# Attention loop: values a step later, split maxima turned a step later still, weight pieces off GpSimd, threshold operations spread over groups

## The reference

```
attention, 32 heads of 16:
  x  -> chunks of 64 tokens; subtract (max+min)/2 per channel and chunk;
        8 scale classes by the channel maximum; round to int4
  Q, K, V = that @ int4 weights + bias;  probs = softmax(Q K^T);  ctx = probs V
  ctx -> the same chunks, thresholds (cmax > tmax / 2^k), classes, int4 rounding
  out = that @ int4 Wo + bias
cross attention with one energy matrix per batch (ctx_1024, Wq, Wk)
ffn: three matrices of 2048 x 512, each made ternary:
  w_int = clip(round(w / mean|w|), -1, 1);  down(silu(gate) * up)
```

## Time and profile before

| what | us |
|---|---|
| median of 3 runs | 1165.96 (1163.58 to 1167.1) |
| the profiled execution, its own time | 1173.1 |
| its span, first to last instruction | 1171.2 |
| the attention loop in it, about | 130 to 637 |
| PE, DVE, ACT, POOL busy in the whole span | 950.5, 877.4, 660.0, 389.5 |

### The profile page before, as it was taken

One profiled execution on the slowest core, in us unless ns is written; L12 is line 12 of the kernel. 1 busy time (PEld: TensorE's weight loads), 2 busy tenths in 40 slices (PEclk: granted clock), 3 DMA queues, 4 the chain that ended last, 5 costly groups with the idle time before them and its releaser, 6 DMA issues. The chain is left out here.

```text
span 1171.2 us, 13391 instructions
## 1 busy us (share of the span) xinstructions
PE 950.5 (81%) x4075; PEld 367.2 (31%) x4128; DVE 877.4 (75%) x1630; ACT 660.0 (56%) x1091; POOL 389.5 (33%) x303
## 2 busy tenths in 40 slices
PE   3657689899989788988897678896998789889765
PEld 1223222222222222222222343343444344443322
DVE  7996588888889978999892658758746775577347
ACT  3777467777777677766665033355424553365352
POOL 4103355566665775663002323150005001400000
PEclk9788799999999999999999878999999999999977
DMA  8865545655565554546433112330234014202400
GB/s 322 337 235 197 179 145 163 182 182 177 173 180 180 159 157 153 176 143 169 125 117 102 59 72 46 71 100 0 56 79 117 1 38 98 45 1 61 109 11 36
DMA packets 90684, 145.00 MB, mean 124 GB/s; under 512 B 12339, under 2 KB 52147, under 8 KB 89078
## 3 DMA queue, kind: packets, MB, share of 16 engines
q1 hardware_dynamic: 90614, 144.16, 40.7%
HBM read 84.75 MB, written 42.21 MB: 108 GB/s over the span
## 5 line engine op out<-in xcount | busy, mean ns | idle before, releaser
L1278 DVE TENSOR_REDUCE neg_max<-banks 128x1 f32<-128x512 f32 x512 | 331.3, 683 | 47.7 <-PE banks L1130 44.4
L1238 ACT ACTIVATE probs<-banks 128x512 f32<-128x512 f32 x512 | 278.0, 599 | 115.2 <-PE banks L1151 114.2
L1130 PE MATMUL banks<-k_st,q_st 96*128 96x512 bf16 x512 | 196.2, 388 | 21.6 <-DVE neg_max L1278 19.2
L1151 PE MATMUL banks<-q_st,k_st 99*128 99x512 bf16 x512 | 194.2, 382 | 15.2 <-ACT probs L1238 10.3
L1544 POOL TENSOR_TENSOR rstd<-vare,half 128x1 f32<-128x1 f32 x48 | 28.1, 586 | 390.4 <-DVE vare L1536 390.4
L1165 PE MATMUL banks<-probs,v_st 128*32 128x512 f32 x1024 | 136.2, 604 | 17.4 <-ACT pv_z L1251 16.2
L1766 PE MATMUL banks<-q_T,f_int_all 128*128 128x512 bf16 x493 | 125.2, 395 | 17.6 <-DVE h_ring L1787 11.3
L1130 PEld LDWEIGHTS banks<-k_st,q_st 96*128 96x128 bf16 x512 | 50.1, 98 | 170.5 <-DVE neg_max L1278 106.1
L1781 ACT ACTIVATE h_ring<-h_ring 128x512 f32<-128x512 f32 x64 | 40.3, 630 | 104.8 <-DVE h_ring L1776 104.8
L1776 DVE TENSOR_TENSOR h_ring<-banks,gate_row 128x512 f32<-128x512 f32 x64 | 44.1, 689 | 60.9 <-PE banks L1766 60.0
L1400 POOL TENSOR_SCALAR woT<-woT 128x1024 f32<-128x1024 f32 x24 | 87.5, 3645 | 2.9 <-ACT woT L1394 1.0
(11 more groups left out here) (270 smaller groups left out, 1512.6 us busy)
## 6 DMA issues: line engine op xcount, KB each, us to landing
f_int_all<-in_ffn_dram SPq DMA_DIRECT2D x24, 512.0 KB, 8.2
qk_parts<-parts SPq DMA_DIRECT2D x32, 384.0 KB, 2.6
q_st<-qk_parts SPq DMA_DIRECT2D x32, 384.0 KB, 3.9
k_st<-qk_parts SPq DMA_DIRECT2D x32, 384.0 KB, 4.9
woT<-in_ffn_dram SPq DMA_DIRECT2D x24, 512.0 KB, 3.4
qk_parts<-parts SPq DMA_DIRECT2D x32, 256.0 KB, 2.9
pv_rows<-pv_z SPq DMA_DIRECT2D x32, 256.0 KB, 5.0
hz<-h_turned SPq DMA_DIRECT2D x32, 256.0 KB
```

What stands on the lines that cost most here:

```text
L1130: pe.matmul(s_bank[(16 * g.n + tile) % SB], q_st[g.i][0:KR, j, qt * P:(qt + 1) * P], k_st[g.i][0:KR, j, :], start=True, stop=True).then_in ...
L1151: pe.matmul(st_bank[at % STB], k_st[g.i][:, j, kt * P:(kt + 1) * P], q_st[g.i][:, j, :], start=True, stop=True).then_inc(st_mm, 1)
L1238: act.activation(probs[ktp][:, j, i, :], st_bank[(16 * g.n + 2 * w + i) % STB], ACT.Exp).then_inc(exp_done, 2)
L1278: dve.tensor_reduce(neg_max[:, g.h, tile:tile + 1], s_bank[(16 * g.n + tile) % SB], AX.X, ALU.max, negate=True).then_inc(max_done, 1)
```

## The change

- `PV_AT` becomes (2, 3, 6, 7): the first two quarters of the values come one step later. `pe_nm` moves from the end of u1 to the end of u2, and the copy of nm_T from after u2 to between the two maxima of u3.
- A weight piece is clipped by DVE in u5 of its own period (`dve_ffn`), and MAGIC is taken off by ACT after the exps and `act_pv` of u0 of the next period (`act_ffn_store`, with a new constant `neg_magic`). POOL has no part in it. SP issues the next load right behind the nm_T transfer.
- `dve_levels` runs in u1, u3, u5, u7 of r=0 and u1 to u7 of r=1; `pool_scale` in r=2 behind that period's parts; `act_round` in u1, u3, u5, u7 of r=3; `dve_n` at (3, u7), (4, u0), (5, u1), (5, u6).

```
-            PV_AT, QK_AT, V_AT, HIGH_AT, MIDDLE_AT = (1, 2, 6, 7), (3, 5), 5, (4, 6), (5, 7)
+            N_AT = ((3, 7), (4, 0), (5, 1), (5, 6))
+            PV_AT, QK_AT, V_AT, HIGH_AT, MIDDLE_AT = (2, 3, 6, 7), (3, 5), 5, (4, 6), (5, 7)
...  pe_period
-                    if u == 1:
+                    if u == 2:
...  act_period
-                    if g.b > 1 and g.r == 3 and 1 <= u <= 4:
-                        act_round(act, g.b - 2, u - 1)
+                    if g.b > 1 and g.r == 3 and u % 2:
+                        act_round(act, g.b - 2, u // 2)
                     if u == 3 and g.n < PIECES:
                         act_ffn(act, g.n)
+                    if u == 0 and 0 < g.n <= PIECES:
+                        act_ffn_store(act, g.n - 1)
...  dve_period
-                    if u == 2:
-                        dve.wait_ge(nm_mm, g.n + 1)
...
+                        if u == 3 and i == 0:
+                            dve_nm_T(dve, g)
                     if g.h == 0 and u in QK_AT and g.has(2):
                         dve_y(dve, g.tile(2), QK_AT.index(u))
+                    if u == 5 and g.n < PIECES:
+                        dve_ffn(dve, g.n)
                     dve_context(dve, g, u)
...  dve_context
-                    else:
-                        dve_levels(dve, g.b - 2, u - 1)
-                if g.b > 1 and g.r == 1 and u < 4:
-                    dve_levels(dve, g.b - 2, 7 + u)
-                if g.b > 1 and g.r == 3 and u > 4:
-                    dve_n(dve, g.b - 2, u - 5)
-                if g.b > 1 and g.r == 4 and u == 0:
-                    dve_n(dve, g.b - 2, 3)
+                    if u % 2:
+                        dve_levels(dve, g.b - 2, u // 2)
+                if g.b > 1 and g.r == 1 and u:
+                    dve_levels(dve, g.b - 2, 3 + u)
+                if g.b > 1 and (g.r, u) in N_AT:
+                    dve_n(dve, g.b - 2, N_AT.index((g.r, u)))
...  pool_period
-                if g.n < PIECES:
-                    pool_ffn(pool, g.n)
-                if g.b > 1 and g.r == 1:
+                if g.b > 1 and g.r == 2:
                     for ct in range(KD):
                         pool_scale(pool, g.b - 2, ct)
...  sp_period, behind the nm_T transfer
+                if g.n + 1 < PIECES:
+                    sp_ffn(sp, g.n + 1)
...
+            def dve_ffn(dve, c):
                 raw = f_ring[:, c % 2, :]
+                need(dve, "f_round", c + 1)
+                did(dve.tensor_scalar(raw, raw, MAGIC - 1.0, MAGIC + 1.0, ALU.max, ALU.min), "f_clip")
+
+            def act_ffn_store(act, c):
+                need(act, "f_clip", c + 1)
+                did(act.activation(f_int_all[:, c, :], f_ring[:, c % 2, :], ACT.Identity, bias=neg_magic[:]), "f_done")
```

More of the change, by code:

```diff
@@ L71, in decoder_layer @@
         magic = keep("magic", [P, 1])
+        neg_magic = keep("neg_magic", [P, 1])
         chunk_of = keep("chunk_of", [96, NB, S], BF16)
@@ L736, in _ @@
                 def _(pool):
+                    pool.memset(neg_magic[:], -MAGIC)
                     pool.memset(onesf[:], 1.0)
@@ L1294, in dve_nm, with dve_nm_T @@
                     dve.tensor_tensor(nm3[:, 2, :], nm_f[:], nm3[:, 1, :], ALU.subtract).then_inc(nm3_ready, 1)
+            def dve_nm_T(dve, g):
+                dve.wait_ge(nm_mm, g.n + 1)
+                if not g.first:
+                    p = g + -1
+                    dve.wait_ge(nm_in[p.i], 16 * (p.round + 1))
+                dve.tensor_copy(nm_T[:], misc.bitcast(BF16)[0:48, 0:P]).then_inc(nm_T_ready, 1)
             def dve_period(dve, g):
@@ L1378, in sp_period @@
                     sp_rsums(sp, g.n // 2 - 2)
-                if g.n + 1 < PIECES:
-                    sp_ffn(sp, g.n + 1)
                 if g.n == PIECES:
-                    need(sp, "f_done", 2 * PIECES)
+                    need(sp, "f_done", PIECES)
                     load_wo(sp, woT[:], bo_row[:])
@@ L1388, in sp_ffn @@
             def sp_ffn(sp, c):
-                need(sp, "f_done", 2 * (c - 1))
+                need(sp, "f_done", c - 1)
                 sp.dma_start(f_ring[:, c % 2, :], io["ffn"][c]).then_inc(f_in[c % 2], 16)
@@ L1395, in act_ffn @@
                                    scale=f_rec[:, c // FPW:c // FPW + 1]), "f_round")
-            def pool_ffn(pool, c):
+            def dve_ffn(dve, c):
                 raw = f_ring[:, c % 2, :]
[L1399 to L1402, removed]
+                need(dve, "f_round", c + 1)
[3 more added lines that the diff above has]
+                did(act.activation(f_int_all[:, c, :], f_ring[:, c % 2, :], ACT.Identity, bias=neg_magic[:]), "f_done")
             def groups(eng, period):
```

## The result

The changed kernel takes 1172.41 us in the median of 12 runs (1166.92 to 1177.24), the kernel before 1165.99 (12 runs). The ratio is 1.0056, 95% interval 1.0036 to 1.0076: slower by 0.6%, where 1155 was forecast.

A forecast was written before the change was run, and what follows sets the result against it. PE and DVE, each about nine tenths busy, were taken to bound the attention loop, feeding each other through three banks. Plain pairs +4, context -15.2: -11 from 1173.1 gives 1162, less 7 for the median: 1155; range 1140 to 1170.

The forecast's parts named there:

- the prices of clip and store: Time of the two new operations: clip on DVE 0.69 us, store on ACT 1.15 us, 24 of each.
- the stop at u2 behind the store: In u2, PE's second turned tile waits for u1's first exp, behind ACT's store, until about 4.0 us; without store 2.9.
- the plain pair of 30.1: Even and odd period without context work: 15.5 and 14.65 us, a pair 30.1 against 29.7 before.
- PE's waits of turned tiles for exps: Expected in the profile after: PE's turned tiles wait for exps some 25 us more in total than before.
- The pair with the scalings: Pair of 36.54 us: scalings behind POOL's parts remove waits of 3.77 on ACT and 2.92 on DVE; 31.1, so -5.4.
- Loads. ... SP waits in r=5 ... Nothing.: SP's queue: earlier weight loads cost nothing; spread and sums go out some 5 us later, their readers a period away.
- Ten plain pairs.: Batches 0, 1 and second half of 2, counted as ten pairs without context work: +4 us in all.
- The lock: DVE's faster-mode operations and POOL's exclude each other; the even-period clip waits 1.16, 0.9 reaches PE, ten times: +9 us.
- the slower rival: The rival "the store on ACT decides", 1173 us, chance 0.18; the lock works in its direction.
- The context pairs ... -15.2.: Pairs with context work and the last three periods: -2.2, -5.4, -2.7, -3.9 and -1.0, sum -15.2 us.
- the fixed 1.0 for DVE's excess: In the 33.33 us pair: about 1.0 us on a plain pair's 30.1 where DVE is over its share, giving 31.1.
- the store on ACT decides: Rival: u3 starts no earlier than 5.99, moved values add 1.09 in about 20 plain periods: +22, total 1173; chance 0.18.

## Why the prediction was wrong

The sign was wrong, and the measured 1172.4 lies outside the range of 1140 to 1170.

Right were the prices of clip and store; the stop at u2 behind the store (the tile at 3.97, forecast 4.0; moving the store brings it to 2.93 in even periods, forecast 2.9, but only to 3.47 in odd ones); and from there the whole even and odd period (15.48 and 14.65, forecast 15.5 and 14.65), so the plain pair of 30.1. The forecast said that the plain pairs would be slower than before and that the context would pay it back almost fourfold. The first held: 3.3 us over seven pairs. PE's waits of turned tiles for exps were said to grow by some 25 us; they grew from 9.6 to 14.3.

The pair with the scalings came out at 29.8 (forecast 31.1), for a reason the prediction had wrong in part. It put the stall down to the place of the scalings, ahead of the parts. With the pieces off POOL and the scalings where they were, the pair is 30.61 and 29.58, and with the scalings moved and the pieces on POOL it is 35.96. What made POOL late were the weight pieces.

By first maxima the loop up to the last score tiles takes 486.6 us, the kernel before 473.8, and the forecast's own pairs add up to 461.5. The gap of 25.1 is made of the two pairs with an r=6 (7.3), the last period (6.9), the four context pairs (6.3), 2.5 more in the last three periods and the pair of 32.23 (2.1); the seven other plain pairs give nothing. So these steps of the sum were wrong:

*"Loads. ... SP waits in r=5 ... Nothing."* It is the last period's 19.0 us against 12.1: 6.9 us. I followed spread and sums to their readers and stopped there. Behind them in SP's queue stood a load of 1 MB, which slid right in front of nm_T. The cost was what the wait pushed together in the queue, not what it made late: without the load in front the period is 12.05.

*"Ten plain pairs."* Two of them hold an r=6 and the changed kernel is there, against the kernel before, 3.1 us longer (15.55 to 18.69) and 2.4 (15.55 to 18.00) in one period each. The lock was in the prediction, as a part of the slower rival, at 0.9 us ten times; in fact it struck the clip in two of those periods, with 2 us of waiting in PE each and then the lower clock. It also struck a cast in the pair of 32.23, where the prediction had no POOL operation in view. I had not put `dve_bias`, six operations that only r=6 has, into the steps.

*"The context pairs ... -15.2."* Beside the 29.8, they gave 32.8, 33.9 and 32.0 where 31.1, 30.0 and 30.0 were said, and the last three periods are 40.8 even without the 6.9, where 38.3 was said. The level steps moved into r=1 filled that period (16.1 us in batch 3, against 13.7); the fixed 1.0 for DVE's excess, taken from no row, was too small. What each operation of a level pair costs there I have not taken apart.

The rival that came nearest is "the store on ACT decides", by the size of the effect: moving the store is worth 1.1%. Its condition, u3 no earlier than before, did not come about (5.35 against 5.99), so that its 1173 is close to the measured 1172.4 is luck. In the traces the change is slower by the steps above, on top of a store that turned a gain of the later values into a small loss. In time, the store's place is clear of the noise, and so is the early n_T on top of spreading alone (1.0112 to 0.9993); on top of the changed kernel the early n_T and the clip's place are shown by their periods only, and all three together by the ratio of 0.9849. A part is left open: the timed medians differ by 6.4 us where the two traces' loops differ by 12.1, and neither how often the loss in r=4 strikes nor which course the rest of the kernel takes is known for the timed runs.

## What to carry to other kernels

When a wait is moved in a queue that issues transfers, list what stands behind it by size and ask which urgent small transfer each large one now lands in front of. When an operation is put between others in an in-order loop, put it where its engine's consumer is waiting for something else anyway: the same store went with a gain in the old order, and with the new one cost 1.1% more in u0 than in u2. Replay the unusual periods (here r=6), not only the plain one. And a part of a change that fails alone may need the one that gives it room: the later values took a plain pair from 29.6 to 29.9 us by themselves, and from 28.9 to 28.5 once the pieces were off POOL and the store in u2.

## What the runs showed of the hardware

- Operations of DVE that started 0.04 to 0.2 us behind a TENSOR_TENSOR of POOL on 128x512 lasted until about its end or beyond it: the clip took 1.52 instead of 0.68, a 128x16 cast 1.25 instead of 0.17; the 128x32 operation on c_cmax, behind the next one, took 1.13 (0.18 in the kernel with the clip in u4). The order of starting, 0.2 us either way, decided whether the clip or POOL waited. By the Trainium skill (page SBUF — State Buffer, section Who interferes with whom) it is issue order and not the operation's shape that decides; the traces agree for the clip and the cast. That the other engine is shut out to the end does not hold for every operation of POOL: in the kernel before, during its clip of 3.63 us (275.86 to 279.49), a cast of DVE begun at 276.33 took 0.59, and the small operation at 277.44 took 0.16.
- A wait of PE of 2.0 us was followed by 3.4 us at a granted clock of 0.51, one of 5.4 us by 6.5 us at 0.50 (621.32 to 627.79), the lower level of 1.2 GHz. In them the eight value matmuls took 1.65, partly at the higher level, and 1.94 instead of 1.07. So a stall can cost more than its length.
- The nm_T transfer of 12 KB let its tile go 2.35 us after its issue with no large load right in front (611.81 to 614.16), and 5.85 us after it behind a load of 1 MB issued 0.5 us before on the same queue (615.47 to 621.32).
